# A transformer layer with conditioning on one core: new orders for the first and the last round, and moved set-up work

## The reference, cut to what matters

```python
a_alpha = (t @ attn_alpha_w.T)[:, None, :]
x = x + a_alpha * _attention(_ada_rmsnorm(x, t, attn_gamma_w, attn_beta_w), W_q, W_k, W_v, W_o)
f_alpha = (t @ ffn_alpha_w.T)[:, None, :]
x = x + f_alpha * _swiglu(_ada_rmsnorm(x, t, ffn_gamma_w, ffn_beta_w), gate_w, hidden_w, out_w, out_b)
...
out = (input - mean) * jax.lax.rsqrt(var + EPS) * weight + bias
tar_bias = jnp.tanh(convInfo @ lin_w.T + lin_b)[:, None, :]
out = out + tar_bias
return out * weight + bias
```

## Time and profile before

| what | value |
|---|---|
| median of three runs | 539.78 us |
| the profiled execution | 542.6 us |
| its span, first to last instruction | 540.8 us |
| TensorE busy | 503.1 us (93%) |
| VectorE busy | 392.4 us (73%) |
| ScalarE busy | 247.4 us (46%) |
| GpSimd busy | 241.3 us (45%) |
| TensorE's share of the chain that ended last | 78% |
| mean granted TensorE clock | 0.970 |

### The profile page before, as it was taken

How to read it: one execution, slowest core, us unless ns; L and a number is a source line. 1 busy time by engine, 2 the same in 40 slices (tenths; PEclk the granted TensorE clock), 3 DMA queues, 4 the chain that set the end, 5 groups by cost and what they waited for, 6 DMA issues and landing times.

```text
span 540.8 us, 11679 instructions
## 1 busy us (share of the span) xinstructions
PE 503.1 (93%) x4512; PEld 416.4 (77%) x4512; DVE 392.4 (73%) x792; ACT 247.4 (46%) x354; POOL 241.3 (45%) x165
## 2 busy tenths in 40 slices
PE   7966899999999999999999999999999999998990
PEld 4654777788788978798788978788888978776890
DVE  5588887578876788488876888488875886575636
ACT  2464474327444473537443562537453663422330
POOL 3334374264245443664255453663255441624362
PEclk9867999999999999999999999999999999998996
DMA  7470181003502080103302070204302060301021
GB/s 204 159 183 15 39 199 42 1 1 77 120 1 82 0 190 5 59 19 95 99 0 78 0 194 0 74 3 115 79 0 78 0 156 1 80 1 40 0 79 39
DMA packets 30650, 35.22 MB, mean 65 GB/s; under 512 B 1824, under 2 KB 28704, under 8 KB 30624
## 3 DMA queue, kind: packets, MB, share of 16 engines
q1 hardware_dynamic: 30624, 34.86, 24.7%
HBM read 26.27 MB, written 4.39 MB: 57 GB/s over the span
## 4 chain that ended last, share of the span: by engine, by line
PE 78%; DVE 9%; ACT 4%; POOL 3%; issue 2%; DMA 2%; SPq 1%; ACTq 0%; POOLq 0%; DVEq 0%
PE banks L583 30%; PE banks L606 17%; PE banks L414 7%; PE banks L506 6%; PE banks L533 4%; PE banks L444 3%; PE banks L519 3%; PE banks L524 2%; DMA final<-outb_in 2%; PE banks L554 1%; DVE work_c L1045 1%; DVE act_t L1094 1%; PE banks L508 1%; PE banks L399 1%; DVE qpar L1025 1%
## 5 line engine op out<-in xcount | busy, mean ns | idle before, releaser
L583 PE MATMUL banks<-x2s,gh 128*128 128x512 f32 x768 | 193.0, 400 | 5.9 <-DVE act_t L1094 4.5
L583 PEld LDWEIGHTS banks<-x2s,gh 128*128 128x128 f32 x768 | 139.7, 188 | 41.0 <-DVE act_t L1094 5.9
L1276 POOL TENSOR_TENSOR hs<-act_t,hs 128x512 fp32r<-128x512 f32 x64 | 83.0, 1298 | 127.2 <-ACT hs L774 127.1
L606 PE MATMUL banks<-wout,hs 128*128 128x256 f32 x768 | 105.0, 286 | 0.9 <-POOL hs L1276 0.8
L606 PEld LDWEIGHTS banks<-wout,hs 128*128 128x128 f32 x768 | 97.3, 188 | 7.2 <-issue 3.3
L1045 DVE RECIPROCAL work_c<-banks 128x512 f32<-128x512 f32 x16 | 53.7, 3358 | 48.7 <-PE banks L519 48.7
L774 ACT ACTIVATE hs<-act_t 128x512 fp32r<-128x512 f32 x64 | 40.3, 629 | 77.2 <-DVE act_t L1098 73.4
L767 ACT ACTIVATE act_t<-banks 128x512 f32<-128x512 f32 x64 | 38.2, 597 | 61.7 <-PE banks L583 60.3
L1094 DVE SCALAR_TENSOR_TENSOR act_t<-act_t,banks 128x512 f32<-128x512 f32 x64 | 43.9, 687 | 30.1 <-ACT act_t L767 28.7
L781 ACT ACTIVATE pt<-banks 128x1024 f32<-128x1024 f32 x32 | 32.8, 1024 | 50.9 <-PE banks L508 48.1
L506 PE MATMUL banks<-qpair,kpar 64*128 64x128 f32 x512 | 50.3, 317 | 0.5 <-DVE negmax L1037 0.5
(11 more groups left out here) (123 smaller groups left out, 690.5 us busy)
## 6 DMA issues: line engine op xcount, KB each, us to landing
xtok<-x_in SPq DMA_DIRECT2D x8, 512.0 KB, 5.2
work_c<-xn SPq DMA_DIRECT2D x16, 256.0 KB, 3.6
row_aa<-rows_dram SPq DMA_DIRECT2D x16, 256.0 KB, 6.9
xres<-x_in SPq DMA_DIRECT2D x8, 512.0 KB, 7.1
row_af<-rows_dram SPq DMA_DIRECT2D x16, 256.0 KB, 6.8
shift<-rows_dram SPq DMA_DIRECT2D x16, 256.0 KB, 4.3
y<-final SPq DMA_DIRECT2D x7, 512.0 KB, 3.3
x2n<-wqkT_in SPq DMA_DIRECT2D x1, 512.0 KB, 5.2
```

What stands on the lines that cost most here:

```text
L583: last = mm(banks[:, base + part, :], gh[:, a, k, w:w + P], x2s[:, b, k, :], start=(n == 0), stop=(n == 5))
L606: last = mm(banks[:, t // 2, D * (t % 2):D * (t % 2) + D], hs[:, c % 2, b, P * t:P * t + P], wout[:, a, c, :], start=False, stop=(c == CH ...
L1276: tt(hs[:, c % 2, 1, :], act_t[:, c % 2, :], hs[:, c % 2, 0, :].bitcast(F32), ALU.subtract)\
```

## The change

Start: WARM_TABLES and WARM_WEIGHTS go. `linw` is loaded fourth, under a semaphore of its own, and TensorE's `setup_rows` waits for that alone. Round 0 gets a function of its own (`first`) on TensorE: twelve passes (WARM_MAX, three times four) stand around the third and fourth `scores_for_max`, WARM_OUTPUT becomes 8 and writes bank 2, and the second half of the attention uses banks 0 and 1 (`banks_of_o`), so `attend(0, 1)` waits for no normalisation. `setup_outb` and `finish_shift` trade places on VectorE, and the scratch of `setup_outb` becomes x2n. Rounds 1 to 6 keep their order.

Round 7 gets a function `last` on each engine, with another order: outputs of the feed-forward of group 6 are made later, chunks 5 to 7 of it alternate between two pairs of banks, all of chunks 5, 6, 7 and the output chunks 3 to 6 stand behind the attention, and one output chunk behind the last group's first gate chunk. WARM_NORM goes. The residual of the last group stays in PSUM, its statistics are taken from there, and the finish is three tiles on VectorE (LAST_DVE) and one on ScalarE and GpSimd.

TensorE, SyncE and names:

```diff
-LD_SHIFT = 16 * 5
+LD_SHIFT = 16 * 4
...
-WARM_LOADS, WARM_TABLES, WARM_WEIGHTS, WARM_OUTPUT, WARM_NORM = 3, 2, 2, 6, 6
+WARM_LOADS, WARM_MAX, WARM_OUTPUT = 3, 4, 8
+LAST_DVE = 3
...
+        def banks_of_o(g, h):
+
+            return (0, 1) if h and not later(g) else (6, 7)
...
             sp.dma_start(cond, condT).then_inc(ld_tables, 16)
+            sp.dma_start(linw, linT).then_inc(ld_linw, 16)
             load_stage(0)
             load_stage(1)
-            sp.dma_start(linw, linT).then_inc(ld_lin, 16)
             for dst, src in ((lnw_b, lnw), (lnb_b, lnb), (linb_b, linb), (outb_b, outb_dram)):
                 sp.dma_start(dst, src.to_broadcast([P, D])).then_inc(ld_lin, 16)
             load_stage(2)
...
-                if t < TT // 2:
-                    sp.wait_ge(last_dve, TT // 2 + t + 1)
+                if t < LAST_DVE:
+                    sp.wait_ge(last_dve, LAST_DVE + t + 1)
                 else:
-                    sp.wait_ge(last_pool, 2 * (t - TT // 2) + 2)
+                    sp.wait_ge(last_pool, 2 * (t - LAST_DVE) + 2)
...
+                if h and later(g):
                     pe.wait_ge(o_steps, 4 * g + 2)
-                else:
+                if not h:
                     pe.wait_ge(v_ready, 4 * g + 4)
                 for j in range(J):
...
+                    last = mm(banks[32 * j:32 * j + 32, den_bank, :], cst[:, C_BLK:C_BLK + 32], pt[:, :, j, :],
                               start=True, stop=True)
                 last.then_inc(den_mm, 1)
                 for b in range(SEQ):
                     for j in range(J):
...
+            def first():
+
+                k_proj(0)
+                q_proj(0)
+                v_proj(0)
+                scores_for_max(0, 0)
+                scores_for_max(0, 1)
+                pe.wait_ge(qpair_ready, 4)
+                pe.wait_ge(q_ready, 4)
+                for n in (2, 3):
+                    warm_up(wqk[:, 0, 0], WARM_MAX)
+                    scores_for_max(0, n)
+                warm_up(wqk[:, 0, 0], WARM_MAX)
+                pe.wait_ge(max_ready, 4)
+                pe.wait_ge(identb_ready, 2)
+                transpose_max(0)
+                for n in range(3):
+                    scores(0, n, alternate=True)
+                attend(0, 0)
+                scores(0, 3, alternate=True)
+                attend(0, 1)
+                transpose_x(1)
+                warm_up(wqk[:, 0, 0], WARM_OUTPUT, 2)
+                o_proj(0)
...
+            def last(g):
+
+                f = g - 1
+                gate_hidden(f, 0)
+                scores_for_max(g, 0)
+                scores_for_max(g, 1)
+                gate_hidden(f, 1)
+                scores_for_max(g, 2)
+                scores_for_max(g, 3)
+                gate_hidden(f, 2)
+                pe.wait_ge(max_ready, 4 * g + 4)
+                transpose_max(g)
+                ffn_out(f, 0)
+                scores(g, 0)
+                ffn_out(f, 1)
+                scores(g, 1)
+                ffn_out(f, 2)
+                attend(g, 0)
+                scores(g, 2)
+                gate_hidden(f, 3)
+                scores(g, 3)
+                gate_hidden(f, 4)
+                attend(g, 1)
+                ffn_out(f, 3)
+                gate_hidden(f, 5, alternate=True)
+                o_proj(g)
+                gate_hidden(f, 6, alternate=True)
+                ffn_out(f, 4)
+                gate_hidden(f, 7, alternate=True)
+                transpose_x2(g)
+                ffn_out(f, 5)
+                ffn_out(f, 6)
+                gate_hidden(g, 0, alternate=True)
+                ffn_out(f, 7)
+                gate_hidden(g, 1, alternate=True)
+                for c in range(2, CH):
+                    gate_hidden(g, c, alternate=True)
+                    ffn_out(g, c - 2)
+                for c in range(CH - 2, CH):
+                    ffn_out(g, c)
...
             zeros = vblk[:, 0:2].rearrange("p b j e d -> p (b j e d)")
             warm_up(zeros, WARM_LOADS)
             setup_tables(FIRST_TABLES)
-            warm_up(zeros, WARM_TABLES)
...
             setup_rows()
-            warm_up(zeros, WARM_WEIGHTS)
-            head(0, norm2=False, ln=False)
-            pe.wait_ge(identb_ready, 2)
-            main(0, fed=False)
+            first()
...
-            main(GROUPS - 1, more=False)
-            ffn_out(GROUPS - 2, CH - 2)
-            ffn_out(GROUPS - 2, CH - 1)
-            transpose_x2(GROUPS - 1)
-            warm_up(wqk[:, 0, 0], WARM_NORM, 2)
-            for c in range(2):
-                gate_hidden(GROUPS - 1, c, alternate=True)
-            for c in range(2, CH):
-                gate_hidden(GROUPS - 1, c, alternate=True)
-                ffn_out(GROUPS - 1, c - 2)
-            for c in range(CH - 2, CH):
-                ffn_out(GROUPS - 1, c)
+            last(GROUPS - 1)
```

ScalarE (`last` and `scale_x3`, whose source may now be PSUM) and VectorE:

```diff
+            def last(g):
+
+                f = g - 1
+                for c in range(3):
+                    feed(f, c)
+                    if c == 0:
+                        place_v_swapped(g)
+                    if c == 1:
+                        keep_x2(f)
+                exp(g, 0)
+                exp(g, 1)
+                scale_x3(g - 2)
+                exp(g, 2)
+                tanh(f, 3)
+                exp(g, 3)
+                o_split(g, 0)
+                hidden_hi(f, 3)
+                tanh(f, 4)
+                tanh(f, 5, 4)
+                o_split(g, 1)
+                hidden_hi(f, 4)
+                hidden_hi(f, 5)
+                tanh(f, 6)
+                tanh(f, 7, 4)
+                hidden_hi(f, 6)
+                x2_split(g)
+                hidden_hi(f, 7)
+                for c in range(CH):
+                    feed(g, c, 2 + 2 * (c % 2))
+                    if c == 1:
+                        keep_x2(g)
+                    if c == 4:
+                        scale_x3(g - 1)
+                scale_x3(g, range(LAST_DVE, TT), banks[:, 0:2, :].rearrange("p a (t n) -> p (a t) n", t=2))
...
-                hi, lo, masked = (x2[:, i, :] for i in range(3))
-                V.memset(x2[:, 3, 0:P], 1.0).then_inc(outb_steps, 1)
+                hi, lo, masked = (x2n[:, i, :] for i in range(3))
+                V.memset(x2n[:, 3, 0:P], 1.0).then_inc(outb_steps, 1)
...
-            def sums_x3(tiles=range(TT)):
-                for t in tiles:
-                    V.bn_stats(stat[:, t, :], final[:, t, :]).then_inc(ln_stats, 1)
+            def sums_x3(x3):
+                for t in range(TT):
+                    V.bn_stats(stat[:, t, :], x3[:, t, :]).then_inc(ln_stats, 1)
...
             def normalise(g, h):
+                o_bank, den_bank = banks_of_o(g, h)
                 dve.wait_ge(den_mm, 2 * g + h + 1)
                 if h == 0:
                     dve.wait_ge(v_ready, 4 * g + 4)
-                V.reciprocal(work_c[:, 0, :], banks[:, 7, :]).then_inc(o_steps, 1)
+                if h:
+                    dve.wait_ge(o_steps, 4 * g + 2)
+                V.reciprocal(work_c[:, 0, :], banks[:, den_bank, :]).then_inc(o_steps, 1)
                 dve.wait_ge(o_steps, 4 * g + 2 * h + 1)
                 dve.wait_ge(o_mm, 2 * g + h + 1)
                 if h:
                     dve.wait_ge(o_hi, 2 * g + 1)
                     dve.wait_ge(o_lo, 2 * g + 1)
-                V.tensor_tensor(work_c[:, 1, :], banks[:, 6, :], work_c[:, 0, :], ALU.mult).then_inc(o_steps, 1)
+                V.tensor_tensor(work_c[:, 1, :], banks[:, o_bank, :], work_c[:, 0, :], ALU.mult).then_inc(o_steps, 1)
...
+            def residual2(f, in_place=False):
...
-                V.tensor_tensor(final[:, :, :], y, x2c[:, :, :], ALU.add).then_inc(x3_steps, 1)
+                V.tensor_tensor(y if in_place else final[:, :, :], y, x2c[:, :, :], ALU.add).then_inc(x3_steps, 1)
...
             def finish_last(f, tiles):
 
+                x3 = x3_banks()
                 for t in tiles:
-                    V.scalar_tensor_tensor(out=final[:, t, :], in0=final[:, t, :], scalar=mv[:, t, 0:1],
+                    if t == TT // 2:
+                        dve.wait_ge(ln_scaled, TT * f + TT - LAST_DVE)
+                    V.scalar_tensor_tensor(out=x3[:, t, :], in0=x3[:, t, :], scalar=mv[:, t, 0:1],
                                            in1=w2[:, :], op0=ALU.subtract, op1=ALU.mult).then_inc(last_dve, 1)
...
                     dve.wait_ge(last_dve, n + 1)
-                    V.scalar_tensor_tensor(out=final[:, t, :], in0=final[:, t, :], scalar=nt1[:, 1, 1, t:t + 1],
+                    V.scalar_tensor_tensor(out=final[:, t, :], in0=x3[:, t, :], scalar=nt1[:, 1, 1, t:t + 1],
                                            in1=shift[:, t, :], op0=ALU.mult, op1=ALU.add).then_inc(last_dve, 1)
...
                 rsqrt_both(1)
-                setup_outb()
+                finish_shift()
...
-                finish_shift()
+                setup_outb()
...
+            def layer_norm(f, n, x3=final):
+
```

(66 more changed lines are left out.)

172 lines of the change are left out of this document (52 added, 120 removed).

## The result

The changed kernel takes 536.37 us (median of 7 runs, 535.3 to 536.83) against 539.78 for the kernel before (7 runs, 538.7 to 542.19): a ratio of 0.9935 [0.9917, 0.9953]. It is faster by 3.4 us, not by 13.65, and lies outside the range of 522.0 to 531.5. Its profiled execution took 536.37 us as well, so its rows and its median are the same case; that of before stood 2.8 above its median. Between the two profiles the span fell by 6.3 us, from 540.8 to 534.5.

What follows compares the result with a forecast made beforehand. TensorE fills the middle rounds, so gains lie at the ends, with VectorE bounding part of the first round. Start 5.85, last round 6.6 and tail 1.2 sum to 13.65: 542.6 to 528.95, less 2.8 gives 526.1; range 522.0 to 531.5.

Steps and rivals of the forecast that it cites:

- The 28.9: First round: VectorE's second statistics start at 28.9 instead of 34.83, 5.95 us earlier, after the freed start.
- the shift row, taken at 5.4: First round, VectorE: three shift row operations beside GpSimd take 5.4 us; uncontended bound about 1.3.
- The price of nothing for the twelve passes: First round, TensorE: passes ahead of the maxima fit beside VectorE's reductions and cost nothing, at most 2.8 us.
- its 2.14 us: First round: the second reciprocal no longer waits 2.14 us for its denominators; part of normalising 8.8 us earlier.
- alone it costs 2.1 us, with GpSimd adding betas and cutting at that time ... about 5.2, as the 6.0 before: Bias arithmetic moved ahead of q's copies of round 1: 5.2 us beside GpSimd, so q_out starts at 65.65.
- 5.85: First round's gain at the second gate chunk, carried through the loop: 5.85 us, bounds 3.5 and 8 for placement alone.
- the last round's 6.6: Last round: its own first output chunk ends 6.6 us earlier from an unchanged start; bounds 5 and 7.3.
- Denominators at 464.3: Last round: denominators of attention's second half come at 464.3 against 471.07, with fewer chunks ahead.
- 10.3 us of waits and warm-ups: Last round before the change: 59.0 of 69.3 us is work, so 10.3 us are waits and warm-ups.
- Contention and clock eat half the start: Rival, chance 0.17: K projection at the lower clock and costlier bias arithmetic; gain 7.5 to 11, about 530.5.
- The start is freed fully: Rival, chance 0.14: short shift row, gap before the projection closes, clock holds; gain 16 to 20, about 521.5.
- Slower: Rival, chance 0.03: without the removed passes the clock stays low in first-round matmuls; 544 if all 18 us run so.

Runs made afterwards that it cites:

- h3: Changed kernel with the old start put back (both early groups of passes, linear weights' load in its old place): 541.68 us, ratio 0.9989.
- g3: Changed kernel without the twelve passes around the maxima: 536.2 us, ratio 0.9865.
- h4: Changed kernel with the second half of the first attention in banks 6 and 7 again: 536.73 us, ratio 0.9898.
- g1: Changed kernel with the bias arithmetic between the halves of group 0's q copies and the shift row in round 1: 526.74 us, ratio 0.9702.
- e2: Changed kernel with bias arithmetic and shift row back in their old places: 531.68 us, ratio 0.9787.
- g2: Changed kernel with fourteen passes in TensorE's idle stretch after the first gate chunk of round 1: 535.16 us, ratio 0.9846.
- g0: Changed kernel run again unaltered: 536.48 us, ratio 0.9879.
- e1: Kernel before, unchanged, profiled once more: 544.62 us, span 542.8.
- h1: Changed kernel with the finish split as before, two tiles on VectorE and two on GpSimd: 536.7 us, ratio 0.9898.
- e4: Changed kernel with the old start and first round, so only the new last round and tail: 538.58 us, ratio 0.9889.
- g5: Changed kernel with the early bias arithmetic, plus four passes ahead of round 7's own first gate chunk: 526.52 us, ratio 0.9713.

## Why the prediction was wrong

**Right: the start and the middle of the first round.** The 28.9 came as 29.18; the shift row, taken at 5.4 by the row it resembled, was 4.9; the projection at the lower clock, the residual's start and the norm's output were within 0.5 us. In part two errors cancelled: VectorE's wait ahead of the residual was 2.04, not 1.2, behind a shift row that was 0.45 shorter. h3 gives the start 5.3 us. The price of nothing for the twelve passes is confirmed by g3, which adds that their use is nothing too. The change of banks stood in the sum with its 2.14 us; they are real and are nearly cancelled by the clock (h4).

**The step that failed: "alone it costs 2.1 us, with GpSimd adding betas and cutting at that time ... about 5.2, as the 6.0 before".** The 2.1 was right (2.2 in g1). The 5.2 was 8.4. I took the price from the block at its old place, where only two of its operations were held up for long (e2: 1.79 and 2.59 us, the next 0.34); at the new place GpSimd does not pause, and all but the MEMSET and one cast are. The prediction counted two kinds of GpSimd work there, betas and the cut of the norm, and left out the cut of a weight stage (2.54 us at 65.69), which stands in the same queue and makes some 2 us of the difference. Both were to be read in the kernel before, at that very place:

```profile
68.75 1.15 DVE L959 TENSOR_TENSOR shift<-shift,final 64x256 f32<-64x256 f32 x1
73.43 2.37 POOL L1281 TENSOR_TENSOR wout<-spare,wout 128x1024 fp32r<-128x1024 f32 x1
```

The shift row's second operation, 0.42 us alone, takes 1.15 beside betas of 1.2, and the cut of the weight stage follows that of the norm without a pause. The miss is 3.2 us, minus 0.3 for an early start, on q_out, ScalarE's pair copies, the tanh and the second gate chunk, all of which were named as waiting. A second item had no price: the gate chunk at the lower clock, 1.6 us. It came with the swap in all eight profiles that have it and in none of the others, e2's among them; but what it costs the whole was not isolated (g2). Together 4.6, of which 0.7 are gone by the transposed maxima of round 1: the loop starts 3.85 later than forecast. e2 shows it by taking the swap away (4.7 us on the median; the first round then gains 6.1 where 5.85 were forecast), g1 by moving the block to where GpSimd rests.

**The second: the last round's 6.6, which measured 3.3.** The mechanism was right, the size was not. "Denominators at 464.3" means 29.9 us from the start of the round; it took 31.4. The single prices from the earlier trace rows were of operations in company that suits them; in this round each of the four scores took 1.47 us where I had 5.4 for four, a gate chunk beside scores 2.97 instead of 2.80. So of the "10.3 us of waits and warm-ups" a part was work, and could not be removed. The second norm was cut 1.9 us late by that and by GpSimd's cut of one hidden chunk (481.09) ahead of the beta it was wanted for. The rest, 1.5 us, is the own gate chunk at the lower clock, which the prediction priced nowhere, though it had priced the same thing in the first round. It comes in half the profiles, but by their times in eleven of the changed kernel's own 13 runs (g0).

**The base.** The sum was made against a profile of 542.6 and then cut by 2.8 to stand to the median. Those 2.8 us were, as far as e1 and h3 tell, the wait for the last small load and the low clock behind it, the very thing that the change removes: the gain counted from the long profile already held them. This is argued: no run of the kernel before near its median was profiled. In the three later sets it had medians of 542.1 to 543.68, so the change is worth 3.4 us by the first set, 7.2 by the set in which both ran again, and 5.7 and 6.4 if its 536.4 is put beside the other two. Of the 10.3 us of error, 7.4 are terms of the sum (3.85, 3.3 and 0.23 in the tail) and 2.8 the base.

**The rivals.** "Contention and clock eat half the start" named the kind (bias arithmetic, clock) but put the clock's fall into the K projection, where the changed kernel's two profiles show 1.00. That fall did come in h4's profile, with the same start, and moved the maxima by 1.7 us. The rival's 530.5 still was 6 us short, since it took the last round as forecast. "The start is freed fully" did not come: the shift row was long, the gap ahead of the output projection 4.77 us, and the clock fell. "Slower" with a clock that stays low did not appear: each fall but the one in the tail was undone.

## What to carry to other kernels

A block of small dependent VectorE operations, here casts and sums, beside a GpSimd queue that never pauses cost about one GpSimd operation for nearly each of its own. Count all that is in that queue at the new place, and put set-up arithmetic where GpSimd rests (2.2 us instead of 8.4, and with the shift row moved too 9.6 us of the whole time in g1). Before a profile is shifted to the median, ask which wait made it long: if the change removes that wait, the shift is counted twice. When a round is said to have so much wait in it, add up that round's own rows, not prices of other rounds. When a small difference of medians is to decide, look first whether the runs of each kernel fall in groups by their mean clock, and compare group with group (h1: 0.3 us by medians, 0.8 by profiles alike).

## What the runs showed of the hardware that was not expected

- In one execution the clock fell although the long idle stretch had been filled: fourteen passes to 70.2 us, then waits of 0.25, 0.94 and 0.72 us, and a chunk at 4.47 instead of 3.06 us (g2). The Trainium skill (TensorE: Matmul & The Clock Gate) ties the lower clock to a whole idle stretch in Part 1, and under A second HAM failure mode: psum-queue depth-cycling tells of a kernel in which frequent short idles between groups of matmuls brought it about. With the second this trace agrees.
- The same instructions with the same two waits ran at the full clock in five profiles and at the lower one in five (2.83 or 4.38 us for eleven matmuls). The K projection of the new start ran at the lower clock for part of its length in one profile alone (7.10 us for 23 matmuls in h4, 5.55 in the changed kernel).
- The start of the kernel before differs from run to run by up to 6 us: its first transposed maxima came at 30.43, 33.56, 35.52 and 36.56 in four profiles with the old loads. The wait for the last small load ended at 16.35 in e4, and in h3 the load was there by 13.36; what makes it land 3 us later in one run than in another was not tried. (With the new start the maxima came between 27.87 and 29.57 in eight profiles, and at 29.05 and 30.20 in g1 and g5, which put the bias arithmetic ahead of them.)
